# A decoder on one core: the causal attention units go from 1024 to 768 columns, and the temperature polynomial goes to VectorE

## The reference, cut to what matters

```
x = x + L1_attn(layernorm(x))      # causal, 16 heads, softmax with its own temperature
x = x + L1_xattn(layernorm(x), ctx, ctx, phi)
x = x + L1_ffn(layernorm(x))       # causal attention with rotary keys (4 key heads), then 8 experts of 512, two per token
```

```
probs   = softmax(logits)                      # with the causal mask
entropy = sum(-probs * log(probs + 1e-9))
poly    = -0.037 e^4 + 0.481 e^3 - 2.3 e^2 + 4.917 e - 1.791
beta    = where(entropy > 0.5, maximum(poly, 1), 1)
out     = softmax(logits * beta) @ v
```

## Time and profile before

| | |
|---|---|
| median of 3 runs | 1427.24 us |
| span of the profiled execution | 1426.1 us |
| its own time beside the span | not given; the runs are 0.5 to 2.8 us above the span |
| TensorE busy | 1279.1 us (90%) |
| VectorE busy | 781.4 us (55%) |
| ScalarE busy | 729.5 us (51%) |
| GpSimd busy | 531.3 us (37%) |

### The profile page before, as it was taken

The page is one execution under the profiler, slowest core; times in us unless marked ns, Lnnn a source line. Parts: engine busy times, 40 slices in busy tenths (PEclk is TensorE's granted clock), DMA queues, the critical chain, the costliest instruction groups (busy, mean ns, idle before and its releaser), DMA issues. The chain is left out here.

```text
span 1426.1 us, 25147 instructions
## 1 busy us (share of the span) xinstructions
PE 1279.1 (90%) x9396; PEld 1061.4 (74%) x9396; DVE 781.4 (55%) x1807; ACT 729.5 (51%) x1297; POOL 531.3 (37%) x745
## 2 busy tenths in 40 slices
PE   9899999989999999996788889888888888999995
PEld 7576776757999999995555656656666556999995
DVE  4886878774111111112665688986877655533332
ACT  6464756652322233221456677778767656444441
POOL 2113040402000000004797888878769223332222
PEclk9999999999999999998998999999999999999998
DMA  9674472901977777822100011010010615322221
GB/s 349 269 184 130 114 183 71 259 25 52 321 259 262 268 268 261 326 105 84 41 1 4 9 42 34 1 38 20 12 38 20 250 55 185 61 43 49 41 44 12
DMA packets 71272, 170.81 MB, mean 120 GB/s; under 512 B 8572, under 2 KB 47489, under 8 KB 61168
## 3 DMA queue, kind: packets, MB, share of 16 engines
q1 hardware_dynamic: 55520, 144.33, 31.5%
q0 software_dynamic: 10224, 16.09, 4.9%
q10 hardware_dynamic: 5408, 8.78, 1.7%
HBM read 122.78 MB, written 48.07 MB: 120 GB/s over the span
## 5 line engine op out<-in xcount | busy, mean ns | idle before, releaser
L1198 ACT ACTIVATE b_ht<-ps,b_b 128x154 f32<-128x154 f32 x256 | 85.3, 387 | 200.5 <-PE ps L1165 187.0
L1213 DVE TENSOR_SCALAR b_yt<-ps,b_b 128x154 f32<-128x154 f32 x64 | 21.2, 373 | 238.8 <-PE ps L1178 238.8
L2353 POOL DMA_INDIRECT experts<-ye,gidx_all x32 | 32.0, 1000 | 319.8 <-SPq L1104 309.3
L1165 PE MATMUL ps<-b_xet,ring 128*128 128x154 f32 x1024 | 141.1, 295 | 1.0 <-DVE b_xet L1206 1.0
L1178 PE MATMUL ps<-b_ht,ring 128*128 128x154 f32 x1024 | 139.7, 294 | 0.4 <-DVE b_yt L1213 0.4
L1178 PEld LDWEIGHTS ps<-b_ht,ring 128*128 128x128 f32 x1024 | 136.3, 189 | 0.6 <-issue 0.6
L1165 PEld LDWEIGHTS ps<-b_xet,ring 128*128 128x128 f32 x1024 | 135.7, 189 | 1.1 <-DVE b_xet L1206 1.1
L2637 POOL DMA_INDIRECT out_dram<-d_yd,d_to x39 | 60.8, 1558 | 146.7 <-DVE d_yd L2605 119.5
L1538 DVE TENSOR_REDUCE c_mx<-ps 128x8 f32<-128x1024 f32 x64 | 77.7, 1214 | 51.9 <-PE ps L1482 51.9
L2586 DVE TENSOR_TENSOR d_g<-d_gs,ps 128x512 f32<-128x512 f32 x37 | 25.4, 688 | 122.3 <-PE ps L2523 122.2
L1477 PE MATMUL ps<-experts 64*128 64x512 f32 x256 | 77.1, 674 | 16.3 <-ACT experts L1574 6.8
(11 more groups left out here) (345 smaller groups left out, 2969.3 us busy)
## 6 DMA issues: line engine op xcount, KB each, us to landing
ring<-in_w SPq DMA_DIRECT2D x64, 1024.0 KB, 5.3
xd<-zero SPq DMA_DIRECT2D x6, 3120.0 KB, 24.8
a_kp<-in_ctx_k SPq DMA_DIRECT2D x8, 1024.0 KB, 17.0
d_xd<-xd SPq DMA_DIRECT2D x39, 130.0 KB, 2.4
xe<-zero SPq DMA_DIRECT2D x1, 4928.0 KB, 35.2
b_xe<-xe SPq DMA_DIRECT2D x32, 154.0 KB
ye<-b_ye ACTq DMA_DIRECT2D x32, 154.0 KB
experts<-in_wd SPq DMA_DIRECT2D x1, 4608.0 KB
```

What stands on the lines that cost most here:

```text
L1165: r = pe.matmul(ps[:, b, CAP * (m % 2):CAP * (m % 2) + CAP], w1r[:, slot, k, P * m:P * m + P], xet[:, e % 2, k, :], start=(k == 0), stop=( ...
L1198: r = a.activation(ht[:, e % 2, m, :], ps[:, b, CAP * (m % 2):CAP * (m % 2) + CAP], ACT.Gelu, bias=b1[:, e, m:m + 1])
```

## The change

The late keys of the early queries are no longer computed. A unit's tile is now 768 columns (`DU`): 512 columns "wide", in which late queries and their two halves of keys and early queries share the rows of four heads, and 256 columns "narrow" for the early queries with the early keys. Whatever reduces or scales per head comes in two parts, wide (4 x 128) and narrow (4 x 64); exponentials, logarithms, the product of two tiles and the copy back stay one instruction of 768 columns.

The scores become six fp32 matmuls of 256 columns and four bf16 mask matmuls, each on a quarter (64 x 64) of the array; the rows of half of the heads hold late queries below and early ones above, or the other way round. The values step becomes eight matmuls of 64 columns with all keys (late queries) and eight of 64 columns with 64 keys (early queries). The copies of the values are three instructions (`head_values`), since every second head has its keys exchanged. The polynomial moves from GpSimd's step "po" to VectorE, behind the entropy sum, in six operations (three `scalar_tensor_tensor` pairs of factors and a maximum). The due times are not changed. The arena's borders move with the smaller tiles.

```
+H2 = P // 2
+WIDE, NARROW = 4 * P, 4 * H2
+DU = WIDE + NARROW
...
+def parts(x):
+    return (x[:, 0:WIDE].rearrange("p (h k) -> p h k", k=P), slice(0, 4)), (x[:, WIDE:DU].rearrange("p (h k) -> p h k", k=H2), slice(4, 8))
+
+def wide(x, of, k):
+    return x[:, of, None].to_broadcast([P, 4, k])
...
+        begin, rows = P * s, [slice(H2 * b, H2 * b + H2) for b in range(2)]
+        late = [ps[rows[b], b0, :].rearrange("p (i a k) -> p i a k", i=2, k=H2) for b in range(2)]
+        early = [ps[rows[1 - b], b0 + 1, 0:NARROW] for b in range(2)]
         for b in range(2):
-            pe.matmul(ps[:, b0 + b, :], l.qt[64 * b:64 * b + 64, ch, P * s:P * s + P], l.kp[64 * b:64 * b + 64, ch, :, P * s:P * s + P],
-                      start=True, stop=False, tile_position=(64 * b, 0), skip_group_check=True)
-        for half in range(2):
-            for b in range(2):
-                row = slice(64 * b, 64 * b + 64)
-                m = pe.matmul(ps[:, b0 + b, :].rearrange("p (h k) -> p h k", k=P)[:, :, 64 * half:64 * half + 64], con["later"][row, P * half:P * half + P],
-                              con["same"][row, :], start=False, stop=True, tile_position=(64 * b, 0), skip_group_check=True)
+            pe.matmul(late[b][:, :, 0:4:3, :], l.qt[rows[b], ch, begin + H2:begin + P], l.kp[rows[b], ch, :, begin:begin + H2],
+                      start=True, stop=True, tile_position=(H2 * b, H2 * b), skip_group_check=True)
+        for b in range(2):
+            pe.matmul(early[b], l.qt[rows[b], ch, begin:begin + H2], l.kp[rows[b], ch, :, begin:begin + H2],
+                      start=True, stop=False, tile_position=(H2 * b, H2 - H2 * b), skip_group_check=True)
+        for b in range(2):
+            pe.matmul(late[b][:, :, 1:3, :], l.qt[rows[b], ch, begin + H2:begin + P], l.kp[rows[b], ch, :, begin + H2:begin + P],
+                      start=True, stop=False, tile_position=(H2 * b, H2 * b), skip_group_check=True)
+        for b in range(2):
+            pe.matmul(early[b], con["later"][rows[b], :], con["same"][rows[b], :],
+                      start=False, stop=True, tile_position=(H2 * b, H2 - H2 * b), skip_group_check=True)
+        for b in range(2):
+            m = pe.matmul(late[b][:, :, 1:3, :], con["later"][rows[b], :], con["same"][rows[b], :],
+                          start=False, stop=True, tile_position=(H2 * b, H2 * b), skip_group_check=True)
...
-        for h in range(NU):
-            m = pe.transpose(ps[:, there.b0 + h // 4, P * (h % 4):P * (h % 4) + P], d[:, h, :], con["ident"])
+        for n in range(DU // P):
+            m = pe.transpose(l.scores(c, g, u)[:, P * n:P * n + P], d[:, P * n:P * n + P], con["ident"])
...
-        for h in range(NU):
-            r, half = h % 4, h // 4
-            m = pe.matmul(ps[32 * r:32 * r + 32, there.bs, P * half:P * half + P], l.vv[:, s, NU * ch + h, :], d[:, h, :],
-                          start=True, stop=True, tile_position=(0, 32 * r), skip_group_check=True)
+        for half in range(2):
+            for r in range(4):
+                pe.matmul(ps[32 * r:32 * r + 32, there.bs, P * half + H2:P * half + P], l.vv[:, s, NU * ch + 4 * half + r, :],
+                          d[:, P * r + H2 * half:P * r + H2 * half + H2], start=True, stop=True, tile_position=(0, 32 * r), skip_group_check=True)
+        for half in range(2):
+            for r in range(4):
+                keys, at_col = slice(H2 * (r % 2), H2 * (r % 2) + H2), WIDE + P * (r // 2) + H2 * (1 - half)
+                m = pe.matmul(ps[32 * r:32 * r + 32, there.bs, P * half:P * half + H2], l.vv[keys, s, NU * ch + 4 * half + r, :],
+                              d[keys, at_col:at_col + H2], start=True, stop=True, tile_position=(H2 * (r % 2), 32 * r), skip_group_check=True)
...
-        v.tensor_reduce(l.mx[u][:, :], both, AX, ALU.max).then_inc(*c.dv.up())
+        for x, of in parts(both):
+            m = v.tensor_reduce(l.mx[u][:, of], x, AX, ALU.max)
+        m.then_inc(*c.dv.up())
...
+def head_values(a, out, src):
+    a.activation(out(slice(0, P), 0), src(slice(0, P), 0), ACT.Copy)
+    a.activation(out(slice(0, H2), 1), src(slice(H2, P), 1), ACT.Copy)
+    return a.activation(out(slice(H2, P), 1), src(slice(0, H2), 1), ACT.Copy)
...
-                v.tensor_reduce(h, e[:, :, :], AX, ALU.add).then_inc(*hr.up())
+                for x, of in parts(e):
+                    m = v.tensor_reduce(h[:, of], x, AX, ALU.add)
+                m.then_inc(*hr.up())
+                p, (other, chosen) = po[u][:, :], (x[:, :] for x in gt[u])
+                v.wait_ge(*hr.at(g, u))
+                v.scalar_tensor_tensor(out=p, in0=h, scalar=FACTORS[0][0], in1=h, op0=ALU.add, op1=ALU.mult)
+                v.scalar_tensor_tensor(out=other, in0=h, scalar=FACTORS[1][0], in1=h, op0=ALU.add, op1=ALU.mult)
+                v.tensor_scalar(chosen, h, -0.5, POLY[0], ALU.is_lt, ALU.mult).then_inc(*c.dv.up())
+                v.wait_ge(*c.dv.now())
+                v.scalar_tensor_tensor(out=other, in0=other, scalar=FACTORS[1][1], in1=chosen, op0=ALU.add, op1=ALU.mult).then_inc(*c.dv.up())
+                v.wait_ge(*c.dv.now())
+                v.scalar_tensor_tensor(out=p, in0=p, scalar=FACTORS[0][1], in1=other, op0=ALU.add, op1=ALU.mult).then_inc(*c.dv.up())
+                v.wait_ge(*c.dv.now())
+                v.tensor_scalar(p, p, 1.0, None, ALU.max).then_inc(*be.up())
...
-        tiles.load_sync(upto_values + two.n_d * NU * P, EXPERTS, tiles.down_loaded)
+        tiles.load_sync(upto_values + two.n_d * DU, EXPERTS, tiles.down_loaded)
...
-               "same": cb[:, 0:256], "later": cb[:, 256:512], "before_bf": cb[:, 512:640], "ones_bf": cb[:, 640:768],
+               "same": cb[:, 0:256], "later": cb[:, 256:320], "before_bf": cb[:, 320:448], "ones_bf": cb[:, 448:576],
```

More of the change, by code:

```diff
@@ L1432, in __init__ @@
         self.qt, self.kp, self.vv = big("qt_" + name, [P, KD, GT]), big("kp_" + name, [P, KD, 4, GT]), big("vv_" + name, [P, GS, NH, 32])
-        self.d = [big("d_%s%d" % (name, u), [P, NU, P]) for u in range(n_d)]
+        self.d = [big("d_%s%d" % (name, u), [P, DU]) for u in range(n_d)]
         self.mx, self.rz = ([sb("%s_%s%d" % (x, name, u), [P, NU]) for u in range(len(UNITS))] for x in ("mx", "rz"))
@@ L1543, in unit @@
             v.wait_ge(*earlier(l.pv, g, u, l.n_d))
-        v.tensor_tensor(l.d[u % l.n_d][:, :, :], both, l.mx[u][:, :, None].to_broadcast([P, NU, P]), ALU.subtract).then_inc(*l.dd.up())
+        for (x, of), (d, _) in zip(parts(both), parts(l.d[u % l.n_d])):
+            m = v.tensor_tensor(d, x, wide(l.mx[u], of, x.shape[2]), ALU.subtract)
+        m.then_inc(*l.dd.up())
         if between is not None:
@@ L1570, in unit @@
             yield from between(u)
-        a.activation(d[:, :, :], d[:, :, :], ACT.Exp).then_inc(*l.ee.up())
+        a.activation(d[:, :], d[:, :], ACT.Exp).then_inc(*l.ee.up())
         yield at("pt", u)
         a.wait_ge(*l.tr.at(g, u))
-        a.activation(d[:, :, :], l.scores(c, g, u), ACT.Copy).then_inc(*l.pt_in.up())
+        a.activation(d[:, :], l.scores(c, g, u), ACT.Copy).then_inc(*l.pt_in.up())
         yield at("os", u)
@@ L1613, in phase_c @@
         x_first = shared("x_first", [P, GS, D])
-        ent, lnp = ([shared("%s%d" % (name, n), [P, NU, P]) for n in range(2)] for name in ("ent", "lnp"))
+        ent, lnp = ([shared("%s%d" % (name, n), [P, DU]) for n in range(2)] for name in ("ent", "lnp"))
         one = Attention(c, sb, "1", (0, 1, 2), 4, shared)
-        upto_queries, upto_mix = arena.used - 4 * NU * P - KD * GT - GS * NH * 32, arena.used
+        upto_queries, upto_mix = arena.used - 4 * DU - KD * GT - GS * NH * 32, arena.used
         ct, phi = ([sb("%s%d" % (name, n), shape) for n in range(2)] for name, shape in (("ct", [P, KD, GT]), ("phi", [P, GS, P])))
@@ L1627, in phase_c @@
         zz, en, po = ([sb("%s%d" % (name, u), [P, NU]) for u in range(len(UNITS))] for name in ("zz", "en", "po"))
-        gt = [[sb("%s%d" % (name, u), [P, NU]) for name in ("square", "other", "chosen")] for u in range(len(UNITS))]
+        gt = [[sb("%s%d" % (name, u), [P, NU]) for name in ("other", "chosen")] for u in range(len(UNITS))]
         x_rot, x_rms = [sb("x_rot%d" % n, [P, GS, D]) for n in range(2)], sb("x_rms", [P, GS, D])
@@ L2052, in rotary_scalar @@
                 a.wait_ge(*two.pv.at(g - 1))
-            for s in range(GS):
-                m = a.activation(two.vv[:, s, :, 0:HD].rearrange("p (g r) e -> p g r e", r=4),
-                                 ps[:, MIX, 4 * HD * s:4 * HD * s + 4 * HD].rearrange("p (g e) -> p g e", e=HD)[:, :, None, :].to_broadcast([P, 4, 4, HD]), ACT.Copy)
-            m.then_inc(*two.v_in.up())
+            head_values(a, lambda part, odd: two.vv[part, :, :, 0:HD].rearrange("p s (g r) e -> p (s g) r e", r=4)[:, :, odd:4:2, :],
```

(3 more changed lines are left out.)

47 lines of the change are left out of this document (19 added, 28 removed).

## The result

The changed kernel takes 1422.1 us in the median of 19 runs (1415.6 to 1429.5), the kernel before 1427.8 in 20 beside them. A twentieth run of the changed kernel took 2065.5 us at a mean granted clock of 0.58, a slow state of the chip, and is left out. The ratio is 0.9959, its 95% interval [0.9945, 0.9973]: 5.8 us faster. I had forecast 1398 us and a range that ended at 1421.

What follows compares the result with a forecast made beforehand. No engine was full: TensorE, 83% busy in the third stretch, waited 89.5 us on a ring of engines in fixed order. Waiting -27, TensorE -5, last load +2.6 made -29.4: 1427.2 to 1398 us, range 1374 to 1421.

Steps and rivals of the forecast that it cites:

- The polynomial: Moved from GpSimd to VectorE: 0.97 us for six operations instead of 2.46; GpSimd loses 77 us, VectorE gains 31.
- way round: One unit's path through the engines in the third stretch: 4.5 us shorter in the first attention, 1.45 from the polynomial.
- The share of 0.3: Chosen part of TensorE's 89.5 us of waiting in the third stretch that would go: 27 us.
- rival B: VectorE takes over at once, the written order returns little; a tenth of TensorE's waiting goes: 1416 us, chance 0.18.
- TensorE's term: Transposes, scores and values steps together -0.08 us a unit, 5 us over 64 units; lower bound -20.
- The sentence on the issue floor: Values step: if starts are at least 25 ns apart, 32 records want 0.8 us, making the forecast 10 us later.
- The elementwise work: Narrower tiles in both attentions save 33 us of VectorE, 44 of ScalarE and 44 of GpSimd.
- The last load: Weight load at the stretch's end grows from 256 to 1536 KB: +2.6 us, bounds 0 and +3.1.
- C: Rival: the ring of engines was all; 0.55 of TensorE's waiting goes: 1376 us, chance 0.08.
- D: Rival: scores and values matmuls on array quadrants do not overlap, TensorE gets busier: 1455 us, slower, chance 0.08.
- E: Rival: the gain is eaten at the stretch's end by the last load or arrival order: about 1427 us, chance 0.05.
- What was to show it: Signs: stretch ends near 1175, VectorE within 10 us, GpSimd -120, ScalarE -38, TensorE's wait about 62, polynomial 1 us.

Runs made afterwards that it cites:

- narrow_only: The changed kernel with the polynomial put back on GpSimd in its own later step, tiles still 768 columns: 1401.9 us, ratio 0.9826 to the kernel before.
- poly_only: The kernel before, tiles still 1024 columns, with only the polynomial moved to VectorE behind the entropy sum: 1453.3 us, ratio 1.0179.
- dve_load: 768-column tiles, polynomial on GpSimd, plus VectorE carrying out the six polynomial operations into tiles nobody reads: 1432.5 us, ratio 1.0017 to the kernel before.
- one_pool: 768-column tiles with the polynomial on GpSimd cut to a single operation (temperature set to 1): 1401.4 us, ratio 0.9831 to the kernel before.
- pair_a: 768-column tiles with the polynomial on GpSimd, timed beside a version with a small last load: 1401.6 us, ratio 0.9818 to the kernel before.
- po_step: The changed kernel with the polynomial on VectorE as its own step, due when it was due on GpSimd: 1408.1 us, ratio 0.9860 to the kernel before.
- load_reduce: 768-column tiles, polynomial on GpSimd, plus six small VectorE reductions with unused results behind the entropy sum: 1405.9 us, ratio 0.9882 to the kernel before.

## Why the prediction was wrong, step by step

- **The polynomial: the step that failed.** The prediction gave it a shorter way round and 31 us of VectorE, and no price on the path, though it said that a delay there "eats what the narrower tiles gave". The move costs 19 us in the changed kernel (narrow_only is at 0.9826, the changed kernel at 0.9959). "Six of them [...] = 0.97 us. Bounds: 0.5 us [...] and 1.3 us": undisturbed it is 1.0 us, as worked out; in the mean it is 1.48, outside the bounds, since I took the durations of small VectorE operations that GpSimd happened not to meet. VectorE is busy 42 us longer than in narrow_only, 47 longer in poly_only than before, not 31. In dve_load the same operations cost 27 us, of which 19 go when their kind no longer stands behind GpSimd. "So the way round gets 1.45 us shorter" is worth nothing that one_pool could show.
- **The share of 0.3, -27 us: failed as well.** In the changed kernel TensorE's waits went from 89.5 to 87.5 us, -2. Even in narrow_only they fell by 8 only, to 81, a tenth of them, which is rival B's share:

```profile
663.90:1173.90 510.00, 428.94 (x4810) 320.37 (x4809) 352.76 (x981) 334.42 (x612) 350.07 (x668) 0.97 0.16 56
```

  That version is 28.7 us shorter in the stretch, near the 29.4 of my sum, but by another split: 20.3 us of it are TensorE's busy time and 8.4 waiting, where I had 5 and 27. That the narrow tiles alone are worth nearly what I forecast for the whole is thus luck: two wrong terms that make up for each other.
- **TensorE's term, -5 us, was mis-sized.** The scores step runs from 1166.75 to 1167.87 in the changed kernel and the values step on to 1168.59:

```profile
1166.75 0.43 PE L1491 MATMUL ps<-experts 64*64 64x256 f32 x2
...
1167.87 0.43 PE L1534 MATMUL ps<-experts 128*32 128x64 f32 x16
...
1168.23 0.43 PE L1539 MATMUL ps<-experts 64*32 64x64 f32 x16
...
1168.59 0.43 PE L1491 MATMUL ps<-experts 64*64 64x256 f32 x2
```

  Scores 1.12 us (1.28 before; forecast 1.18), values 0.72 (0.57 before; forecast 0.81). With the transposes' -0.22 that is -0.23 a unit, 15 us in place of 5, in the direction of the bound of -20. The clock records agree: with the busy time at half clock counted half, TensorE's work in the stretch is 427.1 us before, 413.1 in narrow_only and 412.2 in the changed kernel. So some 14 of narrow_only's 20 us are less work and 6 a better clock, and in the changed kernel's 12.2 us a worse clock takes back 3 of 15. The sentence on the issue floor has a slip: 0.8 us for the values step is 0.23 above the 0.57 of the rows, not 0.4, so by itself the floor asked for no later forecast.
- **The elementwise work was right in the main.** A pair of 512 and 256 columns on VectorE lasts 1.00 to 1.02 us in the median (forecast 1.05), ScalarE's exponential 842 ns and its copy 808 (0.83), GpSimd's product 1820 ns (1.79). The scalings are 1.61 (1.5); the 2.3 ns a column that the forecast named would have made the pair 2.0. VectorE fell by 40 us in narrow_only (forecast 33), ScalarE by 28 (38), GpSimd by 34 (44).
- **The last load was underrated.** Forecast +2.6 us, at most 3.1, with TensorE idle for nearly 4. (1024 KB at 423 GB/s are 2.5 us, not 2.6.) The idle is 4.1, but the chain's wait is 4.4 longer than in rows 9, and the half clock behind the pause, which I had not priced, adds 2.6 in the changed kernel, 2.8 in pair_a and 1.4 in narrow_only.
- **The rivals.** B came nearest in its mechanism: VectorE is awaited, 1416 us, inside my range but not as the likeliest. Its reason held for 8 us of dve_load's 27, and what it lacked was the stall. C fell (one_pool, and a tenth of the waiting in narrow_only where it wanted 0.55). D fell: the quadrants overlap, though the diagonal pair shares a bank. The Trainium skill's "TensorEngine Tiling (Array Packing)", Gotcha 1, by which different row tiles can't use one PSUM bank at once, is not borne out for tiles that write different partitions. E, about 1427, is as near by the number; its mechanism is there, but it is worth only some 5 us of the 24 that are missing.
- **What was to show it.** GpSimd's fall (96 in place of 120), ScalarE's (30 in place of 38), VectorE's even load, the scores step and the idle for the weights came roughly as said. VectorE's load stayed even for a wrong reason: the tiles took 40 us from it and the polynomial gave it 42, where I had 33 and 31. The end of the stretch, the polynomial's 1 us and the waits near 62 did not.

What stays open: how much of the 1% that the later step gives back is order and how much is fewer stalls (7 held operations and 6 us in po_step, 25 and 15 in the changed kernel, by the timeline), and whether the lower clock follows from the pauses alone. That the two go together is seen in poly_only and dve_load, and no run set the clock apart from the waits. What part of the changed kernel's 19 us is stall and what is VectorE's load was not measured; the split is dve_load's.

## What to carry to other kernels

Before a small operation moves from GpSimd to VectorE, ask what GpSimd does at that moment and how many SBUF inputs the operation has: here its mean in place was half as long again as its quiet duration, and 22 us of such stalls cost 19. A shorter dependent chain is worth only what the awaited engine gets back; test it by leaving the chain out (one_pool) before paying for it with another engine's time. When a region that nothing uses any more lies at the end of a load order, fetch it first, not last: here that gave 4 to 6 us. Count a pause of TensorE at more than its length, for the clock behind it (1.4 to 2.8 us here behind a pause of 4 to 5).

## What the runs showed of the hardware

- VectorE's `scalar_tensor_tensor` with two SBUF inputs and its fp32 `tensor_scalar` of 8 columns, 0.15 to 0.17 us alone, stood for up to 1.8 us, until a GpSimd `tensor_tensor` of 256 to 768 columns that had begun before them was done. `tensor_reduce` of the same tiles never did, in 192 instructions of load_reduce.
- Row tiles on diagonal quadrants that write different partitions of one PSUM bank ran side by side: six fp32 matmuls of 256 columns and four masks in 1.12 us, where the step before the change took 1.28.
- 32 matmul records of 64 columns took 0.72 us, 22 ns each with the change of tile shape in it. By the issue floor of 25 ns in the Trainium skill, "TensorE: Matmul & The Clock Gate", section "Wait — 56ns, not 53.3ns?", they would have wanted 0.8; on column tiles side by side it did not hold: within a group of four the starts lie 7 ns apart.
- The same matmuls (3403 and 3402 records) kept TensorE busy for 449.2 us at a mean granted clock of 0.96 and for 462.3 at 0.92.
